# A four-stage transformer kernel: the values' scaling as a two-tensor operation, and other places for projections, routing, gates and sums

## The reference

```python
x = x + L0_attn(ln(x))   # 8 heads; see below
x = x + L0_ffn(ln(x))    # 704 wide, inputs and weights of each linear rounded blockwise to fp4
x = x + L1_attn(ln(x))   # 16 heads of 16, layer norm on q and k, output projection
x = x + L1_ffn(ln(x))    # x W^T + b, plus top-2-of-8 routed low-rank experts (rank 16)
```

```python
scores = einsum('bhqk,bhck->bhqc', q, k).reshape(B*H, C, C)
att = softmax(scores / sqrt(K), axis=1)      # over q
out = einsum('bqhc,bhcd->bqhd', att.reshape(B, C, H, C), v)
```

## Time and profile before

| | us |
|---|---|
| median of 3 runs (3079.7 to 3087.47) | 3085.51 |
| the profiled execution | 3082.79 |
| its span | 3081.0 |
| PE busy | 2617.4 (85%) |
| PEld busy | 1419.5 (46%) |
| DVE busy | 2140.9 (69%) |
| ACT busy | 1962.3 (64%) |
| POOL busy | 1302.4 (42%) |
| mean granted TensorE clock | 0.959 |

### The profile page before, as it was taken

One profiled execution on the slowest core, in us unless ns is written; L12 is line 12 of the kernel. 1 busy time (PEld: TensorE's weight loads), 2 busy tenths in 40 slices (PEclk: granted clock), 3 DMA queues, 4 the chain that ended last, 5 costly groups with the idle time before them and its releaser, 6 DMA issues.

```text
span 3081.0 us, 115296 instructions
## 1 busy us (share of the span) xinstructions
PE 2617.4 (85%) x50158; PEld 1419.5 (46%) x50158; DVE 2140.9 (69%) x4363; ACT 1962.3 (64%) x3701; POOL 1302.4 (42%) x1645
## 2 busy tenths in 40 slices
PE   4866786998889987999889987999889988899796
PEld 3534553445544455444544455444554445444232
DVE  6778766947687577866678486875778666775433
ACT  2541355875578755876568855787558765687683
POOL 4752275216642266224652166323662156411211
PEclk9988899999999999999999999999999999999798
DMA  4212341315214342324324252233323242222311
GB/s 127 56 27 41 65 94 48 71 32 109 72 48 83 60 94 57 73 47 83 90 59 83 45 106 51 59 71 68 94 60 67 44 89 69 64 65 45 84 29 28
DMA packets 474922, 204.69 MB, mean 66 GB/s; under 512 B 287752, under 2 KB 464400, under 8 KB 474392
## 3 DMA queue, kind: packets, MB, share of 16 engines
q1 hardware_dynamic: 472120, 195.12, 30.2%
q10 hardware_dynamic: 2272, 1.85, 0.2%
HBM read 46.61 MB, written 32.51 MB: 26 GB/s over the span
## 4 chain that ended last, share of the span: by engine, by line
PE 42%; DVE 29%; issue 8%; ACT 8%; SPq 5%; DMA 5%; POOL 4%; DVEq 0%; ACTq 0%; POOLq 0%
PE pR L435 18%; PE pV L655 8%; DVE nmaxa L1136 8%; PE pS L435 6%; PE pS L626 5%; ACT ub L880 5%; PE pV L536 3%; PE pR L445 3%; SPq L1803 2%; DMA xT<-ua 1%; DMA xT<-xhb 1%; POOL ua L1596 1%; ACT ua L841 1%; SPq L2000 1%; DVE ua L1048 1%
## 5 line engine op out<-in xcount | busy, mean ns | idle before, releaser
L880 ACT ACTIVATE ub<-pS 128x512 f32<-128x512 f32 x2048 | 1047.6, 611 | 227.5 <-PE pS L626 226.8
L1136 DVE TENSOR_REDUCE nmaxa<-pS 128x1 f32<-128x1024 f32 x512 | 620.8, 1213 | 331.9 <-PE pS L435 329.1
L841 ACT ACTIVATE ua<-pS,nmaxa 128x1024 f32<-128x1024 f32 x384 | 428.0, 1115 | 515.0 <-DVE nmaxa L1136 497.1
L1596 POOL TENSOR_SCALAR ua<-ua,rz 128x256 f32<-128x256 f32 x512 | 494.3, 966 | 490.1 <-DVE rz L1153 445.7
L435 PE MATMUL pS<-ua 128*32 128x512 f16 x8192 | 550.1, 389 | 118.7 <-ACT ua L841 95.1
L655 PE MATMUL pV<-ub,vaug 128*17 128x512 f32 x4096 | 539.4, 600 | 13.6 <-DVE ub L1287 12.8
L626 PE MATMUL pS<-ub 50*128 50x512 f16 x1920 | 351.8, 385 | 28.4 <-DMA ub<-scr 11.5
L435 PEld LDWEIGHTS pS<-ua 128*32 128x32 f16 x8192 | 213.4, 99 | 291.1 <-ACT ua L841 126.2
L435 PE MATMUL pR<-wgu,xT 128*32 128x352 f16 x6144 | 281.3, 318 | 24.7 <-DVE ub L1194 13.4
L536 PE MATMUL pV<-ua 128*32 128x128 f32 x6144 | 250.9, 285 | 59.5 <-DVE oTa L1147 33.8
L626 PEld LDWEIGHTS pS<-ub 50*128 50x128 f16 x1920 | 96.7, 93 | 406.9 <-ACT ub L880 331.5
(11 more groups left out here) (249 smaller groups left out, 4012.9 us busy)
## 6 DMA issues: line engine op xcount, KB each, us to landing
ua<-ua SPq DMA_DIRECT2D x384, 128.0 KB, 2.7
ub<-scr SPq DMA_DIRECT2D x264, 64.0 KB, 2.7
scr<-ub SPq DMA_DIRECT2D x30, 512.0 KB, 3.6
x<-in_L_attn_x SPq DMA_DIRECT2D x8, 1024.0 KB, 5.9
between<-x SPq DMA_DIRECT2D x7, 1024.0 KB, 6.2
ub<-between SPq DMA_DIRECT2D x7, 1024.0 KB, 6.1
out<-ub SPq DMA_DIRECT2D x7, 1024.0 KB, 5.5
ub<-scr SPq DMA_DIRECT2D x192, 32.0 KB, 1.9
```

The source lines that it names most:

```text
L841: e.activation(EA[n % 4], pS[:, 1024 * (n % 2):1024 * (n % 2) + 1024], ACT.Exp, bias=nmaxa[:, n % 32:n % 32 + 1], accum_out=zz[:, n % 8:n ...
L880: e.activation(EB[(4 * n + hl) % 8], pS[:, 512 * hl:512 * hl + 512], ACT.Exp).then_inc(e1_in, 1)
L1136: e.tensor_reduce(nmaxa[:, n % 32:n % 32 + 1], pS[:, 1024 * (n % 2):1024 * (n % 2) + 1024], AXX, ALU.max, negate=True).then_inc(max0_in, 1)
L1596: e.tensor_scalar(vs[m % 4], vv[:, :, 32 * c:32 * c + 32], rz[:, c:c + 1], None, ALU.mult).then_inc(vs_in, 1)
```

## The change

The scaling of the values becomes a tensor-tensor multiplication whose second operand is `rz` read with stride zero, instead of a tensor-scalar one. `project_at` puts the four projections of the third pair one place earlier, on TensorE, ACT and VectorE, and the fills on SP with them (35.6 and 41.6 instead of 36.6 and 42.6); the first two pairs and all other distances stay. The four routing places come 0.5 earlier on three engines. The gates, their exp, the transposes ghT and their high and low parts come 1.0 earlier. The sums are 2.7 apart instead of 2.9, from the same first place. (`0.9 * t` for `.9 * t` in `heads` changes nothing.)

```diff
-        R_AT = (19.5, 22.1, 25.7, 28.5)
+        R_AT = (19.0, 21.6, 25.2, 28.0)
+
+        def project_at(pair, n):
+            return 16 * (pair - 1) + (0, 0, -1)[pair - 1] + 3 * n
...
-                        yield 16 * (pair - 1) + 3 * n + .3
+                        yield project_at(pair, n) + .3
                         project(b, pair, w, jp)
...
-                    yield 36.2 + 1.1 * hf
+                    yield 35.2 + 1.1 * hf
                     u = take(("ghT", b, hf))
...
-                    yield 39.7 + 2.9 * t
+                    yield 39.7 + 2.7 * t
                     u = take(("base", b, t), two=False)
...
-                yield 30.6
+                yield 29.6
                 e.wait_ge(gate_in, gate_at(b, half_) + 1)
...
-                yield 30.15
+                yield 29.15
...
-                yield 31.15
+                yield 30.15
...
-                yield 32.15
+                yield 31.15
...
-                yield 33.15
+                yield 32.15
...
-                yield 34.15
+                yield 33.15
...
-                    yield 37.1 + 1.1 * hf
+                    yield 36.1 + 1.1 * hf
...
-                    yield 40.2 + 2.9 * t
+                    yield 40.2 + 2.7 * t
...
-                    e.tensor_scalar(vs[m % 4], vv[:, :, 32 * c:32 * c + 32], rz[:, c:c + 1], None, ALU.mult).then_inc(vs_in, 1)
+                    e.tensor_tensor(vs[m % 4], vv[:, :, 32 * c:32 * c + 32], rz[:, c:c + 1].unsqueeze(2).to_broadcast([128, 8, 32]), ALU.mult).then_inc(vs_in, 1)
...
-                        yield 16 * (pair - 1) + (4, 10)[w] + .6
+                        yield project_at(pair, 2 * w + 1) + 1.6
```

More of the change, by code:

```diff
@@ L831, in projections @@
                     for n, (w, jp) in enumerate(((0, 0), (0, 2), (1, 0), (1, 2))):
-                        yield 16 * (pair - 1) + 3 * n + .4
+                        yield project_at(pair, n) + .4
                         project(b, pair, w, jp)
@@ L905, in moe_gate @@
                 for hf in range(2) if half_ is None else (half_,):
-                    yield 36.3 + 1.1 * hf
+                    yield 35.3 + 1.1 * hf
                     high(("ghT", b, hf), ght[:, 0, 512 * hf:512 * hf + 512], 1.0, lambda v: v)
@@ L1123, in projections @@
                     for n, (w, jp) in enumerate(((0, 0), (0, 2), (1, 0), (1, 2))):
-                        yield 16 * (pair - 1) + 3 * n + 1.1
+                        yield project_at(pair, n) + 1.1
                         project(b, pair, w, jp)
@@ L1665, in heads @@
                     xb = x[b % 2][:, t, :]
-                    yield 11.6 + .9 * t
+                    yield 11.6 + 0.9 * t
                     e.wait_ge(xh_in["H"], 8 * b + t + 1)
```

## The result

The changed kernel takes 3010.95 us in the median of 4 runs (3004.71 to 3014.76), the kernel before 3082.61 beside it; the ratio is 0.977, with a 95% interval of 0.975 to 0.979. It is 72 us faster. Forecast were 29 us and a range that ended at 3026, so the direction was right and the size too small by more than half. In a later set of runs of the same two kernels the ratio was 0.981 (0.979 to 0.983), which is 59 us; differences between runs of different sets carry that much uncertainty.

A forecast was written before the change was run, and what follows sets the result against it. No engine bounds the kernel; a chain of waits does, with TensorE idle 15.4 us in n = 24 to 47. Scaling 11 plus places 18 give 29 us: 3085.5 - 29 = 3056.5 us, range 3026 to 3087.

The forecast's parts named there:

- signs of being wrong: Group n = 32 to 39 above 28 us, L1596 above 0.75, or the second attention's phases changing length.
- the sum of the places: Six phases with both attentions: gains 6.3, losses 1.8, so 4.5 us each; two thirds kept, 3 x 6 = 18.
- The ring S, max, exp, S: Score matmul, maximum, exp, next score matmul: said to set a floor behind each removed wait, so two thirds were kept.
- the clock: Granted clock, 0.79 over 1161 to 1169: dips may go or appear with waits; 0, bound 10 us over six phases.
- half is won, 1.0: Gates one place earlier: the score matmul at 1161.39 waits 1.98 us; half of it won, 1.0 us a phase.
- Third pair: Projections one place earlier remove TensorE waits of 0.92 us at 1148.48, 1.92 at 1176.69 and 1.02 at 1187.17.
- The chain says how often it isn't: Scaling's gain: 34 us of chain at 0.93 is 36 operations, x 0.30 = 11 us; bounds 0 and 24.
- Routing: Places 0.5 earlier: wins a 1.44 us wait at the last pair, loses 1.8 us a phase at second and third.
- Rival (b): Routing at 21.6 and 25.2 blocks the scores, waits for L1408 above 1.5 us, later groups don't shorten: 3095.5 us; chance 0.09.
- Sums: Sums 2.7 apart, last at 58.6 instead of 60.0: 0 gain, with 0.4 us as bound either way.
- The end of the attention: Scalings queued behind heads' norms on GpSimd: L1703 comes 1.5 us sooner, 0.61 us of wait, counted within the 11.
- Rival (a): Removed waits return at the next score matmul as waits for ACT; a third of the terms, 3077 us; chance 0.20.

The follow-up runs named there:

- The places alone: All moves in place (routing, third pair, gates, sums) with the old scaling, against the kernel before: 3038.3 us against 3078.9, ratio 0.988.
- Without the collision the pair alone: Third pair earlier, GpSimd's bias additions and second low parts of heads moved behind the gates' chain, against the kernel before: 3056.4 us against 3077.4, ratio 0.994.

## Why the prediction was right in its direction and wrong in its size

- **Where to look: right.** The slowest group was the right place, and its idle time and bank waits were what the change removed. Of its signs of being wrong none came.
- **The step that failed: the sum of the places, "4.5 us a phase" and "I keep two thirds, 3 us, x 6 = 18".** The places alone bring 40 us by the medians, 6.7 a phase, more than the terms uncut. The ring S, max, exp, S, for whose sake a third was taken off, took back nothing that the runs show. In n = 32 to 39 of batch 3 the change won 7.3 us: 3.8 of idle time, 1.7 of the clock and 1.5 by the projection that moved one group earlier. For these the sum had 1.92 and 1.0, for the projection 0.92 (the wait that it fills), and for the clock 0 with 10 us over six phases as bound: 3.8, or 2.6 after the cut. The clock alone brought its bound, 1.7 x 6 = 10, in this group (0.94 before and 1.00 after in all six phases); over the six attentions as a whole it rose from 0.97 to 0.99.
- **Gates, "half is won, 1.0": the term that was most too small.** With ghT left in place they bring 15 us alone, 2.5 a phase. The prediction had read the 0.95 us of L1349 and taken it as that operation's cost. It was a collision with GpSimd's L1703, which ran from 1156.05 to 1157.22 and ended 0.07 us before it. That is only 0.7 us of the chain, and over half of it stays when the gates alone move. More stood ahead of the same maximum: VectorE waited 1.19 us for ACT's copy of the projection and took 0.69 for its low part, and only then came the chain:

```profile
1155.74 0.69 DVE L1025 SCALAR_TENSOR_TENSOR ua<-pR,ua 128x512 f16<-128x512 f32 x1 [1.19 <-ACT ua L794]
1156.34 0.95 DVE L1349 TENSOR_TENSOR xhb<-iota,idx 128x64 f32<-128x64 f32 x1
```

  The prediction names this ("no projection's low part waits beside them") and gives it no price. That ghT, moved with the gates, costs all of the 15 us while the projections stay was in no term.
- **Third pair: 0.92 + 1.92 + 1.02 right as waits, wrong as a sum.** The waits went as said. But the terms were summed as if each edit brought its own. Alone the pair brings 0 and the gates with ghT 0; together 36. Without the collision the pair alone brings 21. That an edit can be worthless until another is made was in none of the rivals.
- **Scaling, duration: right** (0.62 forecast, 0.61 measured). **Its gain: 11 forecast; 19 measured alone (9 to 23), 22 to 34 in company of the places.** "The chain says how often it isn't" came out too small. A share of one chain counts only waits on that chain; it doesn't have what a shorter queue does for the work behind it, nor the waits that the moved places would have made. The matmul rows of the waiters' table fell by 21 us alone and by 29 in company, and were the nearer measure.
- **Routing: waits right, balance wrong.** The second and third pair wait 1.57 and 1.56 us, 1.3 and 0.95 more than before (forecast: 1.2 lost at each, 0.6 given back at one), and n = 24 to 31 fell from 24.8 to 23.2 with the routing alone (forecast: 1.44). The balance was to be a loss of 0.4 us a phase; alone nothing is measured, and in company the four places bring 0.1 to 0.5 points. Undoing the first three places wins 8.1 us, 1.35 a phase where 1.8 was forecast, but that the sizes are near is in part luck, since the groups in question give only 0.8 of it. Rival (b) had this wait right and its consequence wrong: it passed its threshold of 1.5 us, but the later groups did shorten.
- **Sums: 0 forecast, 8 us measured.** Where all of it comes from stays open. In the profile of the kernel before, steps 48 to 63 take 36.5 us in two of the six phases and 39.5 in four; with the sums 2.7 apart they take 37.5 in five, and n = 40 to 47 is 0.4 longer. All in all the six attentions give 4 us of the 16 between the two profiles; 10 more lie behind and between them.
- **The end of the attention:** the wait of 0.61 us for the transposed DMA is gone, and the wait of 2.40 for the scaling is 1.70 (at 1177.03). But the last two groups of the six phases got 13 us shorter in the changed kernel, so more was won here than a part of 11.
- **Rival (a):** a third of its terms is 4 and 6 us, not 4 and 4. This changes nothing in the outcome.

## What to carry to other kernels

When every engine's queue is written by hand, edits to places don't add: a piece that moves decides what its neighbours collide with, so pairs of edits have to be tried, and an edit that shows nothing alone is not thereby useless. A small operation that takes four times its usual time may be held by another engine: compare each row with its own kind, and look at what the other engines ran beside it, before taking its duration as its cost. For the worth of a shorter operation look at the waits of its waiters as they stand in the table beside its share of one chain; here, in one kernel, the chain's share was too small. And price the clock in a stretch that loses its waits: it was 10 us in one group here.

## What the runs showed of the hardware

- On GpSimd a scaling of 128 x 256 fp32 by one number for each partition takes 925 ns as TENSOR_SCALAR with a scalar from memory and 614 ns as TENSOR_TENSOR with that number read at stride zero: the form with two tensor inputs is the faster one.
- VectorE's operations with two SBUF operands, 0.22 us long, took up to 1.09 us beside a TENSOR_TENSOR of GpSimd. Beside the same L1740 and L1706 the operations with one operand, L1359 and L1363, took their usual 0.22 and 0.20. The hold goes the other way too: L1706, 1.16 us long with the third pair alone, took 2.16 in the changed kernel at 1135.63, where VectorE's L1373 ran at 1135.27 for 1.49:

```profile
1135.27 1.49 DVE L1373 TENSOR_TENSOR xhb<-xhb 128x1024 f32<-128x1024 f32 x1
1135.63 2.16 POOL L1706 TENSOR_TENSOR ub<-ub 128x512 f16<-128x512 f32 x1
```
